# Twenty-eight feed-forward tiles in the last batch's attention pairs, four whole tiles to a pair, and the ternary weights made in the prologue

## What is computed

```
x = x + attention(layernorm(x)) @ wo
x = x + ffn(layernorm(x))
attention: 16 heads of 32; out = (softmax(q1 k1') - lam * softmax(q2 k2')) @ v, then a norm over each head
ffn:       h = bitlinear(x, w_fc) + gate * (x @ v' @ fast_b' @ u');  out = bitlinear(relu(h)**2, w_proj)
bitlinear: scale = mean|w| of each row;  w is replaced by scale * clip(round(w / scale), -1, 1)
```

## Time and profile before

| | us |
|---|---|
| median of 3 runs | 3834.18 (3832.46 to 3834.82) |
| span of the profiled execution | 3832.1 |
| PE, DVE, ACT, POOL busy | 3758.7, 3175.8, 2822.2, 27.3 |
| prologue, to the first exponential | 99.3 |
| 64 pairs, to 2757.77 | 2658.5 |
| feed-forward with the passage into it | 1074.3 |

### The profile page before, as it was taken

The page is one execution under the profiler, slowest core; times in us unless marked ns, Lnnn a source line. Parts: engine busy times, 40 slices in busy tenths (PEclk is TensorE's granted clock), DMA queues, the critical chain, the costliest instruction groups (busy, mean ns, idle before and its releaser), DMA issues.

```text
span 3832.1 us, 57684 instructions
## 1 busy us (share of the span) xinstructions
PE 3758.7 (98%) x21960; PEld 2078.1 (54%) x21960; DVE 3175.8 (83%) x3070; ACT 2822.2 (74%) x3681; POOL 27.3 (1%) x30
## 2 busy tenths in 40 slices
PE   8999999999999999999999999999899999999999
PEld 6344444444444444444444444333388888888887
DVE  5899999999999999999999999999955555555554
ACT  3889889898988989999898898988733333333333
POOL 0000000000000000000000000000100000000000
PEclk9999999999999999999999999999999999999999
DMA  6444444444444444344344334434110101001010
GB/s 194 111 93 95 94 101 94 94 102 92 99 97 97 93 98 100 93 100 97 92 97 100 91 87 99 106 77 98 45 31 23 44 23 34 33 28 39 22 44 22
DMA packets 213108, 304.70 MB, mean 80 GB/s; under 512 B 90352, under 2 KB 110832, under 8 KB 212272
## 3 DMA queue, kind: packets, MB, share of 16 engines
q1 hardware_dynamic: 212656, 300.31, 32.7%
q10 hardware_dynamic: 128, 0.03, 0.0%
HBM read 180.72 MB, written 117.44 MB: 78 GB/s over the span
## 4 chain that ended last, share of the span: by engine, by line
PE 83%; ACT 10%; issue 3%; DVE 3%; DMA 0%; ACTq 0%; SPq 0%; DVEq 0%
PE ps L661 19%; PE ps L636 15%; PE ps L762 12%; PE ps L743 12%; PE ps L572 10%; ACT pr L1057 7%; PE ps L719 5%; PE ps L575 3%; PE ps L685 3%; DVE acc L1405 2%; PE ps L748 2%; ACT xin L1007 1%; ACT rl L1063 1%; PE ps L796 1%; PE ps L544 1%
## 5 line engine op out<-in xcount | busy, mean ns | idle before, releaser
L1057 ACT ACTIVATE pr<-ps 128x1024 f32<-128x1024 f32 x2048 | 1983.6, 1030 | 235.9 <-PE ps L636 229.6
L1405 DVE TENSOR_TENSOR acc<-acc,pr 128x2048 f32<-128x2048 f32 x752 | 1719.4, 2286 | 45.9 <-ACT pr L1057 16.5
L661 PE MATMUL ps<-pr,vst 128*32 128x512 f32 x8192 | 1017.3, 600 | 0.0
L636 PE MATMUL ps<-qst,kst 50*128 50x512 f32 x4096 | 806.0, 461 | 44.2 <-ACT pr L1057 41.9
L636 PEld LDWEIGHTS ps<-qst,kst 50*128 50x128 f32 x4096 | 342.0, 184 | 724.0 <-ACT pr L1057 540.0
L1215 ACT ACTIVATE rb<-ps,scf 128x512 f32<-128x512 f32 x256 | 176.4, 689 | 395.8 <-PE ps L748 395.8
L661 PEld LDWEIGHTS ps<-pr,vst 128*32 128x32 f32 x8192 | 209.0, 109 | 432.6 <-issue 416.4
L1640 DVE TENSOR_TENSOR sb<-rb 128x512 f32<-128x512 f32 x256 | 177.1, 692 | 273.9 <-ACT rb L1215 271.7
L743 PE MATMUL ps<-yh,tT 128*128 128x512 f32 x1024 | 401.6, 392 | 0.0
L762 PE MATMUL ps<-tP,hh_ 128*128 128x512 f32 x1024 | 398.6, 389 | 0.5 <-DVE hl_ L1645 0.5
L743 PE MATMUL ps<-yl,tT 128*128 128x512 f32 x1024 | 398.5, 389 | 0.0
(11 more groups left out here) (171 smaller groups left out, 3447.7 us busy)
## 6 DMA issues: line engine op xcount, KB each, us to landing
qst<-q_scratch SPq DMA_DIRECT2D x128, 256.0 KB, 4.7
kst<-k_scratch SPq DMA_DIRECT2D x128, 256.0 KB, 7.0
q_scratch<-stg SPq DMA_DIRECT2D x112, 256.0 KB
k_scratch<-stg SPq DMA_DIRECT2D x112, 256.0 KB
qst<-q_scratch SPq DMA_DIRECT2D x128, 128.0 KB, 5.1
kst<-k_scratch SPq DMA_DIRECT2D x128, 128.0 KB, 7.7
vst<-v_scratch SPq DMA_DIRECT2D x128, 128.0 KB, 4.7
xr<-in_L_attn_x_dram SPq DMA_DIRECT2D x64, 256.0 KB
```

The costliest lines, as they stand in the source:

```text
L636: ins = e.matmul(ps[:, 2 * c + hh, :], kst[rows, r, j, t * 128:(t + 1) * 128], qst[rows, r, j, c * 512:(c + 1) * 512], start=True, stop=True)
L661: ins = e.matmul(ps[32 * c4:32 * c4 + 32, 4 + j, :], vst[:, r, t, 32 * hh:32 * hh + 32], pr[:, sl, c, hh, :], start=(t == 0), stop=(t == 7 ...
L1057: e.activation(pr[:, sl, c, :, :], ps[:, 2 * c:2 * c + 2, :], ACT.Exp, scale=SCALE).then_inc(s_exp, 1)
L1405: e.tensor_tensor(acc[:, j, :], old, new, ALU.add).then_inc(s_add, 1)
```

## The change

The ternary weights are made in the prologue. SP loads a unit of 1 MB of w_fc or w_proj (8 units, two buffers `wf0`, `wf1`). ACT takes magnitudes after tile T of `UNIT_AT`, DVE scales and rounds one tile later (`dve_ternary`, in place), ACT takes the sign one tile later again (`act_ternary`), and SP stores it as bf16 and only then loads the next unit into that buffer (`sync_weights` waits for the sign). In pairs 1 to 32 SP turns them with 16 transposing DMAs of 128x1024 and stores them; POOL loads them as fp32 in and after pair 56.

Parts go on to pair 59 with rows of the feed-forward's chunks 0 and 1. Pair 56 carries the low-rank weights. Pairs 57 to 63 carry four ups each (28 of the 256): `UP_PIECES` puts all 9 matmuls of one in each of rounds 0, 2, 3 and 4, and ACT's Relu (`act_early_relu`) stands in the same round, ahead of the round's last exponential. The results go to DRAM and come back in the feed-forward stage, where ACT squares them. PE's last additions go back to DVE, and PE's product with v stands ahead of the scores in all rounds (`late` is gone). Chunk 0 and units 0 to 11 of chunk 1 then have downs only.

```diff
+UP_PIECES = {0: ((0, 0, 9),), 2: ((1, 0, 9),), 3: ((2, 0, 9),), 4: ((3, 0, 9),)}
...
+LOWP = NPAIR - NP
+UPP = LOWP + 1
+NUP = 4 * (NPAIR - UPP)
+MAGIC = 12582912.0
+UNIT_AT = (2, 4, 6, 8, 11, 13, 15, 18)
+TURN_P = 1
...
-    return (P // 4 + 3, P % 4) if P // 4 + 3 < NC else None
+    return (P // 4 + 3, P % 4) if P // 4 + 3 < NC + 2 else None
...
+                e.wait_ge(s_tern, i - 1)
+            dst = wf[i % 2][:].rearrange("p (t e) -> p t e", t=4) if i < 4 else wf[i % 2][:]
             e.dma_start(dst, wsrc[i]).then_inc(s_wf[i % 2], 16)
 
+        def sync_ternary(e, i):
+            e.wait_ge(s_tern, i + 1)
+            e.dma_start(tna[i], tt[:, i % 2, :]).then_inc(s_tna[i % 2], 16)
+
+        def sync_turn_ternary(e, v):
+
+            i, half = divmod(v, 2)
+            e.wait_ge(s_tna[i % 2], 16 * (i // 2 + 1))
+            if v:
+                e.wait_ge(s_tts, 16 * v)
+            e.dma_start_transpose(tu[:], tna[i][:, 1024 * half:1024 * half + 1024]).then_inc(s_tu, 16)
+
+        def sync_turned(e, v):
+
+            i, half = divmod(v, 2)
+            e.wait_ge(s_tu, 16 * (v + 1))
+            dst = ttd[i][:, 8 * half:8 * half + 8, :] if i < 4 else \
+                tpd[:, 8 * half:8 * half + 8, (i - 4) * 128:(i - 3) * 128]
+            e.dma_start(dst, tu[:]).then_inc(s_tts, 16)
...
+        def sync_store_up(e, uu):
+            e.wait_ge(s_rb, uu + 1)
+            e.dma_start(rsc[uu], rbs[:, uu % 2, :]).then_inc(s_rbs[uu % 2], 16)
+
+        def sync_load_up(e, uu):
+            e.wait_ge(s_rbs[uu % 2], 16 * (uu // 2 + 1))
+            if uu >= 4:
+                e.wait_ge(s_sb, uu - 3)
+            else:
+                e.wait_ge(s_sum, 2 * NPAIR - 1)
+            e.dma_start(rbl[:, uu % 4, :], rsc[uu]).then_inc(s_rbl[uu % 4], 16)
...
+            sync_weights(e, 0)
+            sync_weights(e, 1)
             for T in range(24):
                 sync_store(e, T)
+                if T - 2 in UNIT_AT:
+                    i = UNIT_AT.index(T - 2)
+                    sync_ternary(e, i)
+                    if i + 2 < 8:
+                        sync_weights(e, i + 2)
...
+                    if d == 7 and w + 4 < NC + 2:
                         sync_part(e, P)
-                    if d == 7 and P == NPAIR - NP - 1:
-                        sync_weights(e, 0)
-                        sync_weights(e, 1)
-                    if d == 1 and P == NPAIR - NP + 1:
+                    if d == 3 and 0 <= P - TURN_P < 32:
+                        if (P - TURN_P) % 2 == 0:
+                            sync_turn_ternary(e, (P - TURN_P) // 2)
+                        else:
+                            sync_turned(e, (P - TURN_P) // 2)
...
+                    if P >= UPP and d in (1, 3, 4, 5):
+                        sync_store_up(e, 4 * (P - UPP) + (1, 3, 4, 5).index(d))
...
+            for uu in range(4):
+                sync_load_up(e, uu)
+            sync_rows(e, 2)
             sync_post(e, NPAIR - 3, 16)
             sync_post(e, NPAIR - 2, 13)
-            sync_rows(e, 1)
+            for uu in range(4, 7):
+                sync_load_up(e, uu)
...
+            for uu in range(7, 15):
+                sync_load_up(e, uu)
             sync_post(e, NPAIR - 1, 16)
+            sync_rows(e, 1)
+            for uu in range(15, 23):
+                sync_load_up(e, uu)
+            for rt in range(4):
+                sync_out(e, 0, rt)
+            for uu in range(23, NUP):
+                sync_load_up(e, uu)
...
+        def pe_up(e, n, i, bk, n0, n1):
+
+            hi, lo = y_parts(n)
+            for m in range(n0, n1):
+                if m < 8:
+                    t = e.matmul(ps[:, bk, :], tT[:, i, m // 2, :], (hi, lo)[m % 2][:, m // 2, :], start=(m == 0),
+                                 stop=False)
+                else:
+                    e.wait_ge(s_za, 2 * (n + 1))
+                    e.wait_ge(s_zv, 2 * (n + 1))
+                    t = e.matmul(ps[:, bk, :], w2s[:, i * 128:(i + 1) * 128], zt[:, n % 2, :], start=False, stop=True)
+            if n1 == 9:
+                t.then_inc(s_up, 1)
...
+                    e.wait_ge(s_rb, uu - 1)
...
+            pe_up(e, n, i, 6 + a % 2, n0, n1)
...
-                    late = 3 * P + 24 >= 24 * B and d < 6
-                    if gg >= 2 and not late:
+                    if gg >= 2:
                         pe_pv(e, gg - 2)
                     pe_score(e, P, k, 1)
                     pe_score(e, P, k + 1, 0)
-                    if late:
-                        pe_pv(e, gg - 2)
...
+                    if P >= UPP and d in UP_PIECES:
+                        for a, n0, n1 in UP_PIECES[d]:
+                            pe_early_up(e, P, a, n0, n1)
+                    if P == LOWP:
+                        if d == 0:
+                            pe_low_rank_u(e)
+                        if 2 <= d < 6:
+                            pe_low_rank_weights(e, d - 2)
+                        if d == 6:
+                            pe_low_rank_v(e)
+                    if d == 7 and P in (LOWP, LOWP + 4):
+                        pe_low_rank(e, (P - LOWP) // 4)
...
-                    if P > NPAIR - NP and d in TERNARY:
-                        pe_ternary(e, P - (NPAIR - NP) - 1, TERNARY.index(d))
...
-                    pe_up(e, n, i)
+                    if 16 * n + i >= NUP:
+                        pe_late_up(e, n, i)
...
+        def act_magnitudes(e, i):
...
+            if i < 4:
+                for a in range(4):
+                    col, cs = 4 * i + a, slice(a * 512, a * 512 + 512)
+                    t = e.activation(junk[:, cs], wf[i % 2][:, cs], ACT.Abs, accum_out=scf[:, 3, col:col + 1])
+            else:
+                t = e.activation(junk, wf[i % 2][:], ACT.Abs, accum_out=scp[:, 3, i - 4:i - 3])
+            t.then_inc(s_abs, 1)
+
+        def act_ternary(e, i):
+
+            e.wait_ge(s_rnd, i + 1)
+            if i >= 2:
+                e.wait_ge(s_tna[i % 2], 16 * (i // 2))
+            e.activation(tt[:, i % 2, :], wf[i % 2][:], ACT.Sign, bias=magic).then_inc(s_tern, 1)
...
+        def act_early_relu(e, P, a):
+            uu = 4 * (P - UPP) + a
+            e.wait_ge(s_up, uu + 1)
+            if uu >= 2:
+                e.wait_ge(s_rbs[uu % 2], 16 * (uu // 2))
+            else:
+                e.wait_ge(s_vsg[uu], 16 * 2 * NC)
+            e.activation(rbs[:, uu % 2, :], ps[:, 6 + a % 2, :], ACT.Relu, scale=scf[:, 0, uu % 16:uu % 16 + 1]) \
+                .then_inc(s_rb, 1)
...
+                if T in UNIT_AT:
+                    act_magnitudes(e, UNIT_AT.index(T))
+                if T - 2 in UNIT_AT:
+                    act_ternary(e, UNIT_AT.index(T - 2))
+                if T == 22:
                     e.wait_ge(s_wo, 16)
+                    for r in range(2):
+                        e.wait_ge(s_tna[r], 16 * 4)
                     e.activation(woh[:], wos, ACT.Copy).then_inc(s_woh, 1)
...
+                    else:
+                        e.wait_ge(s_rbl[uu % 4], 16 * (uu // 4 + 1))
+                        if uu >= 2:
+                            e.wait_ge(s_hl, uu - 1)
+                        e.activation(sb2[uu % 2][:], rbl[:, uu % 4, :], ACT.Square).then_inc(s_sb, 1)
...
-            if t == 0 or (t == 7 and pe_adds(P, j)):
+            if t == 0:
...
+        def dve_ternary(e, i):
...
+            e.wait_ge(s_scl, 2 * i + 1)
+            e.reciprocal(sc[:, 1, cols], sc[:, 0, cols]).then_inc(s_scl, 1)
+            e.wait_ge(s_scl, 2 * i + 2)
+            for a in range(n):
+                cs = slice(a * 512, a * 512 + 512) if fc else slice(0, HID)
+                t = e.tensor_scalar(wf[i % 2][:, cs], wf[i % 2][:, cs], sc[:, 1, c0 + a:c0 + a + 1], MAGIC, ALU.mult, ALU.add)
+            t.then_inc(s_rnd, 1)
...
+                if T - 1 in UNIT_AT:
+                    dve_ternary(e, UNIT_AT.index(T - 1))
```

655 lines of the change are left out of this document (307 added, 348 removed).

## The result

The changed kernel takes 3856.53 us (median of 4 runs, 3849.74 to 3861.74) against 3833.59 of the kernel before (4 runs, 3832.46 to 3834.82): a ratio of 1.0061, 95% interval 1.0048 to 1.0073. It is slower by 0.6%, where 3815 was forecast. The profiled execution has a span of 3855.8 us, 23.7 over the one before.

A forecast was written before the change was run, and what follows sets the result against it. PE was taken to bound most pairs and feed-forward, DVE and exponentials the last batch. Terms -75.0 + 3.3 + 3.6 + 18.0 + 31 = -19.1 on 3832.1, plus 2.1, gave 3815 us; range 3790 to 3841.

The forecast's parts named there:

- D: Pairs 57 to 63, with four ups each: +18.0 us, bounds +2.6 to +27.
- A: Feed-forward, end of attention to start of chunk 2: -75.0 us, with 80.0 of work and 3.4 of waits.
- B: Pairs 52 to 55 get parts and take as long as mid pairs: +3.3 us.
- F: The 16 transposing DMAs in every second of pairs 1 to 32: 0 us.
- E: Prologue, lengthened by the chain of ternary weight loads, magnitudes and signs: +31 us, bounds +8 to +54.
- The term for the Relu: Pairs 57 to 63: each Relu ahead of an exponential costs 0.2 us, four times a pair.
- The rival that whole tiles cost nothing: Free rounds 1 and 5 give back what rounds 0, 2, 3, 4 owe: total 3797 us, chance 0.12.
- The upper bound, +27: Pairs 57 to 63: the most they would lengthen, in us, with each Relu costing its whole length.
- The rival of late rows: Feed-forward rows from DRAM come too late, four downs taking 9.3 us, not 7.3: total 3829 us, chance 0.06.
- the circle of the prediction: Prologue: sign, issue, landing and magnitudes in a chain, 11.3 or 10.8 us a step, five steps.
- C: Pair 56, without tiles, with a part and the low-rank weights, DVE its limit: 43.5 us, +3.6, bounds +1 to +6.
- the rival on the other side: Transposing DMAs hold SP's queue, delaying the next pair's loads: 3847 us at 2.0 us a transpose, chance 0.10.

The follow-up runs named there:

- the run with pieces: Changed kernel with the same 36 matmuls of four ups cut into pieces over rounds 0 to 5 of pairs 57 to 63: 3829.02 us, ratio 0.9991.
- the run with three edits: Changed kernel with plain copies for transposing DMAs, ups in pieces, early-result loads on POOL, three prologue buffers, magnitudes to `rl`: 3804.85 us, ratio 0.9931.
- the run with all four edits: Changed kernel with ups in pieces, early-result loads on POOL, three prologue buffers, copy of wo in the first pair: 3809.29 us, ratio 0.9942.
- the control: Changed kernel with its 16 transposing DMAs replaced by plain copies of the same bytes, weights left untransposed: 3854.74 us, ratio 1.0063.

## Why the prediction was wrong

The sum's largest failures are two terms put too low: in D the granted clock, put at nothing, and in A the wait, put at 3.4. B and F held, and E held in its mechanism.

**D, the step that failed most.** The term had three parts: PE's demand (+2.6 over the stage before, 290.0 in all), 1.44 a pair lost in rounds 1 and 5, and 0.8 a pair for Relus. The first held: at full clock the 1846 matmuls keep PE busy for 289.5 (the run with pieces). "Nine make about 5.45 and PE is the bound there" held too, at 5.44 on PE. What failed is the rest. Most of it is the clock. All of the earlier trace rows for the pairs showed 1.00, and that was read as a property of the stage; it held for the work as it stood then, and the sum has no term for it. It cost 13.1 us of the 36.9 (302.61 against 289.48; 14.5 if counted by rounds), and 18.9 were missing. The other part is the idle time of rounds 1 and 5, forecast as 5.06 less 4.34 a round, 0.72; PE's work there was 4.37, but its round lasted 5.94, and 1.57 was lost. The 5.06 is a stretch from exponential to exponential, and such a stretch (4.80 here) is not PE's own round. That makes 21.7 us in seven pairs, where 15.7 were forecast under two names, idle time and Relus. The term for the Relu had no ground: no round with an up has a gap on PE, the waits for exponentials stand in rounds 1 and 5, and with the Relu moved the pairs did not get shorter. The rival that whole tiles cost nothing was wrong as well. The upper bound, +27, had whole Relus in it and nothing of the clock; by its own terms it is +29 (42.2 and four times 0.6 a pair), and +36.9 came.

The Trainium skill, "TensorE: Matmul & The Clock Gate", Part 1, has the engine start out throttled and released by activity, so that idle costs matmuls at half rate afterwards. The trace agrees (3.59 against 1.92 us for the same 16 products), and here it stood behind idle pieces of at most 1.2 us in rounds in which PE was busy for 3.2 of 4.8; with that sentence beside the diff, four full rounds next to empty ones would have been a rival.

**A.** The work was right (80.0, and 80.09 measured on POOL's queue); the step that failed is the term of 3.4 for waits, where 16.0 of idle time and 4.2 of lower clock behind it came. The rival of late rows (0.06) was priced by the landing time and the ring of four. The 15.3 us came from the order of SP's queue: loads stood behind `sync_post`, which waits for the last two pairs' products. The order of SP's instructions behind the pairs was in the diff; the term "3.4 of waits" looked at the first load only.

**E.** Five steps from 43 to 98 were forecast; magnitudes 1 ended at 41.6, magnitudes 6 at 97.5, and the transposes began at 103.9 (105.3). That this is so near is in part luck. From issue to magnitudes the loads of units 2 to 6 took 5.9, 6.9, 6.7, 9.4 and 8.8 us, 8.2 more than five times 5.9. Against it, the sign of unit 3 stood ahead of magnitudes 4 on ACT and not behind them, as the circle of the prediction has it, so that the next load was issued (73.05) 2.1 us before they ended (75.17); and the issue took some 0.4 and not 0.9. Behind the transposes' start 30.2 us were needed and not 22.9 + 2: the copy of wo waits for the last two signs' stores (5.9 us), in ACT's order ahead of the last tile's copy. That wait was not in the sum. But the run that moved it gained nothing in the total, and the runs with three buffers still had their first exponential at 122.7 to 125.7, with other waits in place of those for weights. Whether the order, the stores or the DMA engines, 0.88 to 0.94 busy from 60 to 100 us in two of these runs, set the last 23 us over the old 99.3 is not settled.

The Trainium skill, "DMA: Bandwidth & Descriptors", "Anatomy of one DMA — SWDGE (gpsimd) path", fits 2.0 us and the bytes at 436 GB/s to DMAs that GpSimd issues, by which 1 MB takes 4.4 us (an estimate by that page). These loads are SP's, and no load of a unit landed so fast: 5.9 to 9.4 in the chain at a DMA share of 0.76, up to 12.2 in the run with three edits.

**C.** 43.5 was forecast for pair 56; 45.0 to 47.4 came. In the changed kernel PE waited 2.5 us for DVE's `w2s` (L1613), which stands behind two additions of 2.3, and round 3, which held this, took 8.63 at a clock of 0.80 (6.26 at 1.00 in the run with all four edits). The clock had no term here either. The lumps were priced at 1.6.

**B and F** came out as forecast; the rival on the other side, 16 transposing DMAs that hold SP's queue, is excluded by the control (2166.3 against 2167.0 us). The change was slower by other steps.

## What to carry to other kernels

Where a pipeline alternates between two engines in short rounds, give every round its share of the moved work: whole pieces in some rounds leave others to the second engine's pace, and the idle time there is not made up. Don't carry a granted clock of 1.00 over to a changed order of the same work: here gaps of 1.6 us in two of eight rounds cost 3.1 us a pair by themselves, and about 2 more by the clock. Where a stage's clock changes from run to run, look at PE's idle time, which does not, and count the slow rounds. And read a queue's order behind a wait as closely as the transfers' own times.

## What was not expected of the hardware

The granted clock fell within a stage in which PE was still busy 93% of the time (302.61 of 324.33), after rounds with idle pieces of no more than 1.2 us; in the kernel before the same idle time in pieces of at most 0.6 left it at 1.00. It did not fall each time: with the same instructions two to ten of the fourteen rounds behind such a gap were slow, and why one and not another is open. And 0.9 us of repeated matmuls in such a round kept it up: 13 x 0.91 = 12 us of useless work on PE made the kernel about 11 us faster (ratios of 1.0033 and 1.0061 to the kernel before). Of loads of 1 MB, two issued together landed after 8.9 us (median), and the third of three issued together after 12.0.
